# Row sums by transposes on TensorE and a reduction on VectorE, with new hand-written orders, in a two-layer attention and mixture-of-experts kernel

## The reference, cut to what matters

```python
q, k, v = (causal_conv_silu(x @ W.T, conv) for ...)     # 16 heads of 128
q = l2norm(q) * hd ** (-0.5); k = l2norm(k)
def step(state, inp):                                   # over the tokens
    pred = einsum('bhd,bhdv->bhv', kt, state)
    delta = bt[..., None] * (vt - pred)
    state = state + einsum('bhd,bhv->bhdv', kt, delta)
    ot = einsum('bhd,bhdv->bhv', qt, state)
o = o * rsqrt(mean(o * o, axis=-1, keepdims=True) + RMS_EPS) * rms_w
o = o.reshape(b, s, nh * hd) @ Wo.T
```

## Time and profile before

| | us |
|---|---|
| median of 3 runs | 1848.72 (1847.51 to 1849.9) |
| profiled execution, its own time | 1841.73 |
| profiled execution, span | 1839.9 |
| PE busy in the span | 1719.3 (93%) |
| DVE busy | 1442.2 (78%) |
| ACT busy | 1207.0 (66%) |
| POOL busy | 1082.1 (59%) |

### The profile page before, as it was taken

How to read it: one execution, slowest core, us unless ns; L and a number is a source line. 1 busy time by engine, 2 the same in 40 slices (tenths; PEclk the granted TensorE clock), 3 DMA queues, 4 the chain that set the end, 5 groups by cost and what they waited for, 6 DMA issues and landing times.

```text
span 1839.9 us, 43452 instructions
## 1 busy us (share of the span) xinstructions
PE 1719.3 (93%) x14326; PEld 1270.0 (69%) x14326; DVE 1442.2 (78%) x3395; ACT 1207.0 (66%) x2921; POOL 1082.1 (59%) x1144
## 2 busy tenths in 40 slices
PE   5999899999999999999999999999977788888878
PEld 4467567777777777777777777777755466666656
DVE  4322489999999999999999999999945688888853
ACT  1124467777777777777777777777744478778853
POOL 1510057777777777776666656666652377778841
PEclk8999999999999999999999999999976799999999
DMA  9423110110110110100000001000000000000032
GB/s 310 147 82 114 55 30 21 36 30 26 32 34 26 29 34 20 37 23 20 29 14 26 23 17 29 23 17 23 14 1 1 1 1 1 2 1 2 2 86 88
DMA packets 58668, 69.22 MB, mean 38 GB/s; under 512 B 10607, under 2 KB 47231, under 8 KB 58367
## 3 DMA queue, kind: packets, MB, share of 16 engines
q1 hardware_dynamic: 55511, 59.46, 10.9%
q0 software_dynamic: 3072, 8.65, 1.4%
HBM read 51.00 MB, written 17.10 MB: 37 GB/s over the span
## 4 chain that ended last, share of the span: by engine, by line
PE 84%; DVE 7%; ACT 5%; issue 1%; POOL 1%; SPq 1%; DMA 0%; DVEq 0%; ACTq 0%; POOLq 0%
PE banks L689 19%; PE banks L830 6%; PE banks L786 4%; PE banks L805 3%; PE banks L717 3%; PE banks L709 3%; PE banks L701 3%; PE banks L814 3%; PE banks L760 3%; PE banks L642 3%; PE banks L899 2%; PE banks L746 2%; PE banks L754 2%; PE banks L753 2%; PE banks L970 2%; PE banks L661 2%
## 5 line engine op out<-in xcount | busy, mean ns | idle before, releaser
L689 PE MATMUL banks<-xnT,hw 128*128 128x512 f32 x768 | 412.7, 621 | 1.7 <-DVE cv L1824 1.7
L1865 DVE CAST_PREDICATED MM<-lmask,banks 128x512 bf16<-128x512 uint32 x384 | 273.0, 711 | 64.8 <-PE banks L754 42.9
L1348 ACT ACTIVATE T<-banks 128x256 bf16<-128x256 f32 x384 | 147.1, 383 | 226.9 <-PE banks L746 214.2
L1824 DVE SCALAR_TENSOR_TENSOR cv<-banks,hc,cv 128x510 f32<-128x510 f32 (+2 forms) x384 | 277.8, 737 | 4.8 <-ACT cv L1298 4.1
L2368 POOL TENSOR_TENSOR X<-X,yrow 128x512 f32<-128x512 f32 x128 | 161.5, 1283 | 72.7 <-ACT yrow L1380 72.7
L746 PEld LDWEIGHTS banks<-MM,Gb 128*128 128x128 bf16 x1536 | 92.0, 98 | 86.7 <-issue 49.6
L830 PE MATMUL banks<-ho,OT 128*128 128x256 f32 x512 | 143.2, 403 | 0.0
L754 PEld LDWEIGHTS banks<-MM,T 128*128 128x128 bf16 x1536 | 104.2, 98 | 55.7 <-issue 31.9
L1824 DVE SCALAR_TENSOR_TENSOR cv<-banks,hcv,cv 128x510 f32<-128x510 f32 (+2 forms) x192 | 141.2, 735 | 0.8 <-ACT cv L1298 0.7
L2334 POOL TENSOR_TENSOR kn<-nsum,half_pos 128x4 f32<-128x4 f32 x64 | 65.6, 1025 | 126.4 <-DVE nsum L1836 126.4
L754 PE MATMUL banks<-MM,T 128*128 128x64 bf16 x1536 | 136.5, 193 | 0.0
(11 more groups left out here) (321 smaller groups left out, 4918.0 us busy)
## 6 DMA issues: line engine op xcount, KB each, us to landing
MM<-in_eye SPq DMA_DIRECT2D x64, 256.0 KB, 2.6
slot_rows<-zeros SPq DMA_DIRECT2D x1, 5304.0 KB, 20.5
xs<-slot_rows SPq DMA_DIRECT2D x13, 408.0 KB, 3.9
slot_out<-ye SPq DMA_DIRECT2D x13, 384.0 KB, 2.7
hw<-in_hw SPq DMA_DIRECT2D x16, 256.0 KB, 3.5
wgu<-in_wgu SPq DMA_DIRECT2D x1, 2816.0 KB
w1c<-in_ew SPq DMA_DIRECT2D x16, 176.0 KB
X<-in_x SPq DMA_DIRECT2D x4, 512.0 KB, 5.7
```

Of the source, the lines that this page charges most:

```text
L689: ins = pe.matmul(PROJ[t][:], hw[:, kk, t, :], xnT[:, kk, u.b * BLK:(u.b + 1) * BLK], start=(kk == 0), stop=(kk == KD - 1))
L1348: act.activation(strips(T1[:].rearrange("p i t -> p (i t)"), LEVELS[lv], 0, 1), grams_bank(u)[:, 0:TILES * 64].rearrange("p (k e) -> p k e ...
L1824: dve.scalar_tensor_tensor(o, y, taps_of(t)[:, TAPS - 1 - i:TAPS - i], o, ALU.mult, ALU.add).then_inc(dve_conv, 1)
L1865: dve.copy_predicated(dst, m, ps).then_inc(dve_mm, 1)
```

## The change

Three edits go together.

1. The sums of squares. `sums` becomes `turn_squares`: four transposes of the 128 x 128 tiles of `Osq` into one bank. A new step on DVE, `square_sums`, reduces each row of 128 to one number, for four tiles at once. ACT's `mean_squares` now reads that result from `osum` instead of the bank. The column of ones and its fill on POOL are gone. The four transposes have the form of those of `turn_values` (L727), which a unit has already.
2. The `period` lists of PE, ACT, DVE and POOL are written anew. Their start is shifted by some steps, so units are counted one further (`u4` where `u3` stood); beside this some steps trade places.
3. POOL's last periods outside the loop are three instead of two.

```diff
-            def sums(u):
+            def turn_squares(u):
                 pe.wait_ge(act_ot, u.n + 1)
                 pe.wait_ge(pool_osum, u.n + 1)
                 for k in range(TILES):
-                    last = pe.matmul(solve_bank(u)[:, k:k + 1], Osq[:, k, :], ones1[:], start=True, stop=True)
+                    last = pe.transpose(solve_bank(u)[:, k * P:(k + 1) * P], Osq[:, k, :], ident[:])
                 last.then_inc(pe_sums, 1)
...
             def mean_squares(u):
-                act.wait_ge(pe_sums, u.n + 1)
-                act.activation(orr[:, u.b % 2], solve_bank(u)[:, 0:TILES], ACT.Copy, scale=1.0 / HD, bias=Q_EPS).then_inc(act_mean, 1)
+                act.wait_ge(dve_osum, u.n + 1)
+                act.activation(orr[:, u.b % 2], osum[:, u.b % 2], ACT.Copy, scale=1.0 / HD, bias=Q_EPS).then_inc(act_mean, 1)
...
+            def square_sums(u):
+                dve.wait_ge(pe_sums, u.n + 1)
+                dve.tensor_reduce(osum[:, u.b % 2], solve_bank(u)[:].rearrange("p (k d) -> p k d", d=P), AX.X, ALU.add).then_inc(dve_osum, 1)
...
                 do(refine, u3, 0, 0)
+                do(square_sums, u4)
                 do(invert, u2, 2)
...
+                do(rhs_minus, u2, 0, 0)
                 do(add_squares, u3)
-                do(rhs_minus, u2, 0, 1)
...
                 do(gram_rest, u1)
                 merge(i)
-                do(rhs_minus, u1, 0, 0)
+                do(rhs_minus, u2, 0, 1)
...
-            for j in range(3 - 1):
+            LATE = 4 - 1
+            for j in range(LATE):
                 period(NH, j)
```

More of the change, by code:

```diff
@@ L766, in first_solve @@
                     pe.wait_ge(act_last, u.n + 1)
-                    need(pe, act_mean, u.n - 1)
+                    need(pe, dve_osum, u.n - 1)
                     of_inverse(u, c, Bc)
@@ L861, in period @@
[L861 to L872 removed]
+                do(gram_second, u2)
+                do(invert, u3, 8)
@@ new lines, in period @@
+                do(invert, u3, 12)
+                do(invert, u2, 0)
+                do(outputs, u4)
+                do(invert, u2, 1)
+                do(first_solve, u3, 0)
+                do(turn_values, u2)
+                do(invert, u2, 2)
+                do(project, u1, VAL, 0)
+                do(times_gram, u3, 0, 0)
+                do(invert, u2, 3)
+                do(project, u1, VAL, 1)
+                do(correct, u3, 0, 0)
+                do(turn_squares, u4)
+                do(invert, u2, 4)
@@ L2410, in _ @@
             inverse_rms(u)
-            for s in range(2):
-                add_rows(u, s)
+            add_rows(u, 0)
+            add_rows(u, 1)
             for g in range(EARLY + 1, NBLK):
```

164 lines of the change are left out of this document (73 added, 91 removed).

## The result

| | before | after |
|---|---|---|
| median | 1848.12 (4 runs, 1843.70 to 1849.90) | 1935.75 (4 runs, 1926.62 to 1937.00) |
| profiled execution | 1841.73, span 1839.9 | 1936.36, span 1934.5 |
| granted clock, mean | 0.974 | 0.963 |

The ratio is 1.0474, 95% interval 1.0454 to 1.0494: 87.6 us slower, where the forecast said 32. The direction was right; the time lies outside the range.

What follows compares the result with a forecast made beforehand. PE's work was taken to set the 17.87 us period. Merge +35.4 and +1, sums -10.9 and end +6.5 gave +32.0 us on the median of 1848.72, so 1880.7 us; range 1864 to 1896.

Steps and rivals of the forecast that it cites:

- Merge: POOL's row fetch and add, now ahead of `Rm<-bv,Wd`, make PE stand 1.72 us: 30 x 1.18 = +35.4 us, plus 1.
- Gain of the sums: On PE, four transposes replace the products and save 0.40 us; 0.35 us gained in each of 31 units, -10.9 us.
- The reduction in DVE's idle time: DVE's new reduction takes 0.66 to 0.7 us, within 1.6 us idle per unit, so costs nothing in steady attention.
- The end: After the attention, DVE's statistics wait for the last unit's reduction and start 6.5 us later, passed on in full.
- clock gives way: Rival: PE's idle time in merge periods and more transposes bring half clock for part: +51 us more, 1932 us; chance 0.03.

Runs made afterwards that it cites:

- e9: Changed kernel, merge left in place, with 30 memsets ahead of DVE's loop and the half-precision copy made from the bank: 1875.11 us, ratio 1.0156.
- e6: Changed kernel with 30 memsets ahead of DVE's loop and POOL's merge moved ahead of the first `Rm<-bv,Wu`: 1856.24 us, ratio 1.0039.
- e7: e6 with DVE's half-precision copy for chunk 1 made from the bank instead of from `Rf`: 1827.31 us, ratio 0.9879.
- e8: Kernel before with the new sums of squares alone, all old orders and the merge kept: 1888.90 us, ratio 1.0223.
- e12: e7 with DVE's statistics of the first three blocks taken ahead of the last unit's `square_sums`: 1823.13 us, ratio 0.9862.
- e5: Changed kernel with 30 one-element memsets ahead of everything on DVE, shifting its loop: 1899.57 us, ratio 1.0275.

## Why the prediction was wrong

The 87.7 us between first and last `oinv`, taken apart by the runs that follow each other: loop's place 1214.4 - 1174.1 = 40.3 (36.2 by the medians), merge 1174.1 - 1131.4 = 42.7 (43.3), copy 1131.4 - 1107.8 = 23.6 (28.9), and all that is left -18.9 (-22.9).

Against the forecast: its own terms came to 28.2 in e9 where it had 32.0; the copy adds 24.5 and the loop's place 36.2, 88.9 together, and 87.6 was measured. The terms:

- **Merge, +35.4 and 1: right.** POOL's 4.98 us, PE's 1.61 and the period of 19.12 in e9 are the forecast's 5.02, 1.72 and 19.05. Its price shows as 42.7 above because e6 counts it from the new period without a merge, and the forecast counted from the old 17.87; by the forecast's own figures it is 30 x (19.05 - 17.5) = 46.5 in that count, and from e7 to e9 it is 46.1.
- **Gain of the sums, 0.35 us a unit: right for PE's work, but not had.** The four transposes hold PE for 0.45 us, and e7 has the period of 17.46; e6 and the kernel after have 17.85. The first failing step is the gain booked in full because "all of PE's time is on the path", and with it "DVE's work behind the late residual, up to the half-precision copy for the next chunk, is about as long as PE's beside it, which may add 0.1". The copy ends only behind POOL's X add (1.12 us long instead of 0.7), and PE, coming earlier, waits for it: 0.39 us in a unit without a merge, and 0.29 in one with it (19.41 against 19.12), where 0.1 was allowed. It could have been read in the kernel before, where the copy lay within the add and PE already lost 0.12 us to it. Price: 20 to 29 us.
- **The reduction in DVE's idle time, at nothing: right with the new orders** (0.69 us, no wait of PE behind it in e7), but not for the reason given. With the old orders it costs 0.6 us a unit (e8, 18.44), with the same idle time on DVE: what counts is what stands behind the reduction in line, not room on average. The prediction said so of POOL and not of DVE.
- **The end, +6.5: right.** 6.9 us at the statistics, 6.2 at the last normed rows, and 7.0 us given back in e12. From the last `refine` to the end of the span it is 459.5 to 460.0 us in the six profiles with the old end, 462.6 to 468.0 in the nine with the reduction there, and 460.5 in e12.
- **What had no term at all: where the loop lies.** 36 to 40 us, the second failing step. The prediction priced the edits and moves of instructions, and not that the program ahead of DVE's loop became 25 instructions shorter and the loop 6 longer. The rival "clock gives way" touched it from the side: the clock did fall, to 0.97 on average in the stretch 600 to 800, but not from the merges' idle time, which leaves it at 1.00 (e5). In this kernel it took the loop's stall on top of the merge's, and that is why an edge costs 4.3 us among the merges and 1.9 after them.
- **The range** let the unknown costs end at those that had been thought of. Two that had not were 60 us together.

## What to carry to other kernels

Before pricing a change's work, look at whether a hardware loop's place in its engine's program moves: stalls with `issue` as their cause, at a fixed number of units, and more packets on the instruction queue than before, are its mark, and a few dead instructions ahead of the loop are its cure. When an order changes, or the critical engine gets faster, read which of GpSimd's and VectorE's long instructions on on-chip memory lie beside each other, and give the one on the path an operand in a bank. A wait of 0.1 us carries no mark in a timeline: look at the distance between the starts of two products, not only for marks. Put an optional piece of work (a fetch, a merge) where its engine idles longest in a row: here the same merge cost 0.1, 0.8 or 1.5 us by its place.
